# Score constants computed in the keys stage, and keys carried in rounds of three, three and two pieces

## The chip, the cores and the metric

One core of a Trainium2 chip runs the kernel. The metric is the device time of one execution in microseconds, as the median of three runs. The engines are TensorE (PE in the rows, PEld for its weight loads), VectorE (DVE), ScalarE (ACT), GpSimd (POOL) and SyncE (SP), which here issues nearly all DMAs.

## What is computed

A graph attention layer over 128 graphs with 128 nodes and 512 features, of which the first 20 nodes are the keys, with 16 heads of 32 features, in two directions:

```python
vcq = concatenate([v, q_exp], axis=-1)      # q_exp: the graph's condition, zero where a node's row sums to zero
self_feat = vcq @ W_self.T + b_self
for d in range(2):
    A = adj_f if d == 0 else swapaxes(adj_f, 1, 2)
    A = A[:, :, :20, :]
    cond, vb = A.sum(-1), A @ w_bias + b_bias
    kv = self_feat[:, :20]
    qh = (self_feat @ Wq[d].T + bq[d]).reshape(B, N, H, 32)
    kh = (kv @ Wk[d].T + bk[d]).reshape(B, 20, H, 32)
    aff = einsum('bnhd,bmhd->bnhm', qh, kh) / sqrt(32)
    aff = where(cond[:, :, None, :] > 0, aff, NEG) + vb[:, :, None, :]
    w = softmax(aff, axis=-1)
    out_t = einsum('bnhm,bmf->bnhf', w, kv)
    output += einsum('bnhf,hgf->bnhg', out_t, Wout[d]) + bout[d]
return v + relu(output)
```

## The kernel before

Three stages follow each other.

**prepare_weights** (to about 80 us) loads and turns the weights. It folds the query projection into the key side: a_rows holds, for each of 8 units (direction d, group of four heads), the product of Wself and Wq, and cq and bq_all hold what the graph's condition and the bias add to the query of each feature.

**keys_and_values** (about 80 to 372 us) makes the keys and values of all graphs in 8 halves of 16 graphs (320 columns: 16 graphs x 20 keys). Halves 2 to 5 run in a hardware loop (blocks), the others are written out. Per half PE makes 16 projections of 12 matmuls (8 key pieces, 8 value pieces), and between them the sums (8 matmuls) and the four features (48) of the next half. Results go to six PSUM banks in turn: a bank is free when its reader is through (free). ACT empties a key piece into kst, which has two buffers (key_out, L768), and SP stores it to k_dram (L634); ACT empties a value piece into vst (L778, L781), DVE turns it (L703) and SP stores it in four DMAs to v_dram (L640). DVE makes the next half's features (features_out, L669), ACT their high parts (feature_high, L755), POOL their low parts (features_low, L729); DVE turns the nodes of the half after next (turn_x, L75). SP's order in a half is: 8 loads of rows for the half after next (L70), 8 stores of keys, 32 stores of values. In the last half but one, the loads of rows give way to the first loads of the next stage (early_loads).

**window_loop** works off 64 pairs of graphs in slots of some 23 us. A window spans four pairs (8 graphs, 160 columns of keys for a group of heads). In each slot PE generates the mixed keys of two groups of heads for the next window, and computes the scores of four pairs of different age against the present one. generate(t, step) has five steps of 8 matmuls with 32 rows of weights; step 0 (L1540) makes the constants of the scores, from zl, which holds cq and bq_all by columns, and steps 1 to 4 (L1542) the four pieces of the mixed keys. Each step fills the same columns of the four low banks, so these must be emptied before the next: constants_high (ACT, L1432) and constants_low (DVE, L1267) into zc, keys_out (ACT, L1437) into kx. scores(t, a) multiplies the turned nodes xt by kx (L1562) and flags by zc (L1563). Then follow masks on DVE (L1280), maxima, POOL's shift, exponentials on ACT, sums (L1297), normalising, the turn of the weights on PE (turn_weights, L1588; read out by weights_out, L1450), values (L1596) and self_features (L1575). Pair t - 3 is called soft, pair t - 4 late, pair t + 1 nxt. The order of work in a slot is written out by hand for each engine. On PE it is: scores(3), generate 0, scores(2), generate 1, values, scores(1), turn_mask, generate 2, self_features, generate 3, flags, values, scores(0), generate 4, self_features. A matmul in float32 stands in the trace as two records, one in float32r as one.

## Time and profile before

| | us |
|---|---|
| median of three runs | 1914.61 |
| lowest, highest | 1913.51, 1915.31 |
| profiled execution | 1915.0 |
| its span, first to last instruction | 1913.2 |

PE is busy for 1864.9 us of the span, DVE for 1103.0, ACT for 1005.8 and POOL for 725.4. The ends of matmuls are modelled, so the distance from one start to the next tells what a matmul costs, not its length in the row. Idle time of an engine counts only where another waits for it. The mean granted clock of PE is 0.986 of 2.4 GHz.

### The profile page before, as it was taken

How to read it: one execution, taken by the hardware profiler on the slowest of the kernel's cores; microseconds unless marked ns; L12 is line 12 of the kernel's file. 1: busy time of each engine (PE TensorE's matmuls, PEld its weight loads, DVE VectorE, ACT ScalarE, POOL GpSimd, SP SyncE). 2: the span in 40 equal slices, each digit the busy share in tenths (PEclk: the TensorE clock that was granted, in tenths of full speed). 3: DMA queues.
4: the chain of work that ended last, by engine and by line, in shares of the span. 5: the costliest groups of instructions: out<-in, count | busy, mean ns of one | idle time of the engine just before them, and what ended most of it. 6: DMA issues, size and time to landing. Idle time of an engine off the chain costs nothing.

```text
span 1913.2 us, 46955 instructions
## 1 busy us (share of the span) xinstructions
PE 1864.9 (97%) x15864; PEld 1668.7 (87%) x15864; DVE 1103.0 (58%) x1937; ACT 1005.8 (53%) x1717; POOL 725.4 (38%) x617
## 2 busy tenths in 40 slices
PE   8999998879999999999999999999999999999997
PEld 5899998868888888888888888888888888888886
DVE  2433232456666666666666666666666666666632
ACT  2333232235556666666565566555666666656543
POOL 0322222004444444444444444444444444444444
PEclk9999999979999999999999999999999999999999
DMA  6123334444546565555555555565565555555431
GB/s 198 46 83 89 91 96 104 110 115 141 155 137 159 144 156 144 149 144 144 144 144 145 144 157 151 152 154 147 143 159 146 152 142 147 144 145 145 120 93 63
DMA packets 263747, 255.59 MB, mean 134 GB/s; under 512 B 78192, under 2 KB 194160, under 8 KB 263536
## 3 DMA queue, kind: packets, MB, share of 16 engines
q1 hardware_dynamic: 259360, 252.84, 49.4%
q8 instruction: 123, 2.02, 0.4%
q14 instruction: 88, 0.72, 0.1%
q10 hardware_dynamic: 4176, 0.02, 0.1%
HBM read 197.94 MB, written 54.79 MB: 132 GB/s over the span
## 4 chain that ended last, share of the span: by engine, by line
PE 92%; SPq 1%; DVE 1%; issue 1%; ACT 1%; DMA 0%; POOL 0%; POOLq 0%; DVEq 0%; ACTq 0%
PE bank L1562 30%; PE bank L1575 20%; PE low_banks L1542 10%; PE low_banks L828 9%; PE bank L1596 8%; PE bank L828 4%; PE bank L1588 4%; PE low_banks L1540 3%; PE bank L1563 2%; PE bank L1604 1%; SPq L640 1%; ACT kx L1437 0%; DVE zc L1267 0%; DMA k_dram<-kv_kst 0%; SPq L1078 0%
## 5 line engine op out<-in xcount | busy, mean ns | idle before, releaser
L1562 PE MATMUL bank<-kx,xt_main 128*128 128x160 f32 x4096 | 635.9, 304 | 0.3 <-ACT kx L1437 0.3
L1562 PEld LDWEIGHTS bank<-kx,xt_main 128*128 128x128 f32 x4096 | 583.8, 192 | 7.4 <-issue 0.9
L1437 ACT ACTIVATE kx<-low_banks 128x1280 f32<-128x1280 f32 (+3 forms) x268 | 318.2, 1187 | 259.1 <-PE low_banks L1542 259.1
L1388 POOL TENSOR_TENSOR res<-res,xk 128x512 f32<-128x512 f32 x128 | 163.9, 1280 | 669.6 <-ACT res L1427 669.6
L1280 DVE TENSOR_TENSOR sc<-bank,masks 128x320 f32<-128x320 f32 x256 | 125.8, 491 | 398.8 <-PE bank L1563 396.9
L1542 PE MATMUL low_banks<-key_tile,a_rows 32*128 32x160 f32 (+3 forms) x4288 | 220.7, 320 | 14.6 <-ACT kx L1437 8.9
L1575 PE MATMUL bank<-ws_h,xh_main 128*128 128x512 f32 x512 | 222.2, 434 | 2.5 <-DVE res L1306 2.5
L1370 POOL TENSOR_TENSOR sc<-sc,mx 128x640 f32<-128x640 f32 x128 | 160.2, 1272 | 152.1 <-DVE mx L1292 152.1
L1432 ACT ACTIVATE zc<-low_banks 128x1280 fp32r<-128x1280 f32 (+2 forms) x67 | 79.7, 1190 | 244.3 <-PE low_banks L1540 244.3
L1575 PE MATMUL bank<-ws_l,xh_main 128*128 128x512 f32 x512 | 203.1, 397 | 0.0
L1575 PE MATMUL bank<-ws_h,xl_main 128*128 128x512 f32 x512 | 203.0, 397 | 0.0
L1542 PEld LDWEIGHTS low_banks<-key_tile,a_rows 32*128 32x128 f32 x4288 | 157.9, 187 | 51.6 <-DVE zc L1267 16.4
L1364 POOL TENSOR_TENSOR xl_main<-xt_main,xh_main 128x512 fp32r<-128x512 f32 x128 | 162.7, 1271 | 55.1 <-ACT xh_main L1416 55.1
L1563 PE MATMUL bank<-zc,flags 128*128 128x160 f32 x512 | 177.9, 348 | 0.0
L1596 PE MATMUL bank<-vbd,wtt 128*128 128x128 f32 x1280 | 173.9, 283 | 3.8 <-ACT wtt L1450 3.7
L1379 POOL TENSOR_TENSOR wt<-sc,rs 128x640 f32<-128x640 f32 x128 | 163.0, 1273 | 14.1 <-DVE rs L1299 13.6
L1450 ACT ACTIVATE wtt<-bank 128x384 f32<-128x384 f32 (+1 forms) x256 | 111.5, 435 | 108.0 <-PE bank L1588 105.2
L1596 PEld LDWEIGHTS bank<-vbd,wtt 128*128 128x128 f32 x1280 | 152.9, 192 | 15.2 <-issue 14.5
L1306 DVE TENSOR_TENSOR res<-bank,res 128x512 f32<-128x512 f32 x128 | 88.5, 691 | 133.8 <-PE bank L1596 133.8
L75 DVE STREAM_TRANSPOSE xt_main<-rows_main 128x256 f32<-128x256 f32 x256 | 142.8, 619 | 0.0
L1575 PEld LDWEIGHTS bank<-ws_h,xh_main 128*128 128x128 f32 x512 | 96.6, 189 | 38.5 <-issue 20.6
L828 PE MATMUL low_banks<-kv_fh,wkv_h 128*128 128x320 f32 x352 | 110.3, 313 | 7.6 <-ACT kv_kst L768 4.9
(144 smaller groups left out, 3085.4 us busy)
## 6 DMA issues: line engine op xcount, KB each, us to landing
rows_main<-in_x SPq DMA_DIRECT2D x256, 128.0 KB, 6.3
xs<-in_x SPq DMA_DIRECT2D x64, 512.0 KB, 4.8
xk<-in_x SPq DMA_DIRECT2D x64, 512.0 KB, 3.7
res<-c_dram SPq DMA_DIRECT2D x64, 512.0 KB, 7.2
out<-res SPq DMA_DIRECT2D x128, 256.0 KB, 3.1
adj<-in_mask_BxSxSx_ik SPq DMA_DIRECT2D x32, 440.0 KB, 8.2
adj<-in_mask_BxSxSx_ik SPq DMA_DIRECT2D x128, 110.0 KB
vbd<-v_dram SPq DMA_DIRECT2D x768, 10.0 KB
```

The source lines that it names most:

```text
L75: return eng.transpose(dst, src.rearrange("p t (r j) -> p t r j", j=NQ)[:, :, :, j])
L828: mm = nc.tensor.matmul(dst, a(j), b(j), start=(j == 0 and k == 0), stop=(j == C - 1 and k == 2))
L1364: pool.tensor_tensor(xl[:, :, b, :], xt[:, :, p.ring + b, :], xh[:, :, b, :].bitcast(F32), ALU.subtract).then_inc(x_low, 1)
L1370: pool.tensor_tensor(s, s, mx[:, b, :].unsqueeze(2).to_broadcast([P, DIRS * H, NG]), ALU.subtract).then_inc(s_shifted, 1)
L1379: pool.tensor_tensor(wt[:, b, :].rearrange("p (h m) -> p h m", m=NG), sc[:, p.ring + b, :].rearrange("p (h m) -> p h m", m=NG), rs[:, b, : ...
L1388: pool.tensor_tensor(res[:, p.par, b, :], res[:, p.par, b, :], xk[:, p.par, b, :], ALU.add).then_inc(res_ready, 1)
L1437: nc.scalar.activation(taken(kx[:, t.par, j], lo, hi), generated(0, P, lo, hi), ACT.Copy).then_inc(gen_taken, 1)
L1542: mm = nc.tensor.matmul(low_banks[:, r, dst], a_rows[s, o, step - 1, :], rhs, start=True, stop=True)
L1562: mm = nc.tensor.matmul(dst, xt[:, j, p.ring + b, :], kx[:, t.par, j, :, :, w, :].rearrange("p r c m -> p c r m"), start=(j == 0), stop=False)
L1563: mm = nc.tensor.matmul(dst, flags[:, p.ring + b, :], zc[:, t.par, :, :, w, :].rearrange("p r c m -> p c r m"), start=False, stop=True)
L1575: mm = nc.tensor.matmul(OUT[:], a, m[:, j, :], start=(j == 0 and k == 0), stop=False)
L1596: mm = nc.tensor.matmul(OUT[:, 3 * c * DH:(3 * c + SLOTS) * DH], wtt[:, b, c, :], vbd[:, p.par, c, :, b * DH:b * DH + DH], start=False, st ...
```

## The change

The constants of the scores are linear in the keys: per head, the key times the query's bias, and the key times the condition's part of the query, summed over the head's 32 features. The changed kernel computes them in keys_and_values from kst: ACT multiplies a key piece by bq_all (by_biases), POOL by cq (by_conditions), DVE turns both products in blocks of 32 and sums over the 32 features (constant_sums), ACT and POOL split the sums of a half into high and low parts (constants_high, constants_low), DVE turns them (turn_constants), and SP stores them in 8 DMAs per half to z_dram. In the window loop SP loads two small pieces of z_dram per pair into zc (load_constants); flags and nzm follow zc's new layout.

generate has three rounds instead of five steps: pieces 0 to 2, 3 to 5 (12 matmuls each) and 6 and 7 (8 matmuls), where a piece is one of the eight of two groups of heads. The turn of the masks moves ahead of the round of two, place_masks behind weights_out. scores waits for all three rounds at its opening. Of the early loads, those of the edges, of the two edge constants and of xs (load_sum_rows) move to the last half, ahead of its third key store (late_loads), and DVE treats direction 1 of the first edges in the window loop.

```diff
             for p in range(NK):
+                if last and p == 2:
+                    sp.wait_ge(pe_feat, C * HALVES)
+                    sp.wait_ge(f_low, C * HALVES)
+                    v["late_loads"](sp)
...
+            sp.wait_ge(z_turned, n + 1)
+            for r in range(NQ):
+                for e in range(2):
+                    o = Q * r + ZQ * e
+                    sp.dma_start(v["z_dram"][r, e::2, bass.ds(n * HALF, HALF)].rearrange("c (q i) -> q c i", i=Q),
+                                 zt[o:o + MQ]).then_inc(z_stored, 16)
...
+        def constant_sums(n, p):
+            dve.wait_ge(by_bias, NK * n + p + 1)
+            dve.wait_ge(by_condition, NK * n + p + 1)
+            if due(NK * n + p):
+                dve.wait_ge(z_summed, NK * n + p)
+            nc.vector.transpose(pt[:], prod[:, p % 2].rearrange("p k (q i) -> p (k q) i", i=Q)).then_inc(p_turned, 1)
+            dve.wait_ge(p_turned, NK * n + p + 1)
+            if p == 0 and due(n):
+                dve.wait_ge(z_high, n)
+                dve.wait_ge(z_low, n)
+            nc.vector.tensor_reduce(zs[:, p].rearrange("p k q -> p (k q)"), pt[:], AX.X, ALU.add).then_inc(z_summed, 1)
...
                 pick_condition(n + 1)
-            if not last:
                 nonzero(n + 1, 1 - par)
-                for j in range(C):
+            constant_sums(n, 0)
+            for j in range(C):
+                constant_sums(n, 1 + j)
+                if not last:
                     features_out(n + 1, 1 - par, j)
+            constant_sums(n, 5)
             if not tail:
                 turn_x(blk + 1, n + 2, par)
...
                 nc.vector.transpose(vt[:, m % 4], vst[:, m % 2]).then_inc(v_turned, 1)
+                if m < 2:
+                    constant_sums(n, 6 + m)
+            turn_constants(n)
...
+        def by_conditions(n, p):
+            pool.wait_ge(kv_out, 2 * NK * n + p + 1)
+            if due(NK * n + p - 1):
+                pool.wait_ge(p_turned, NK * n + p - 1)
+            pool.tensor_tensor(prod[:, p % 2, 1, :].rearrange("p (b m) -> p b m", m=NG),
+                               kst[:, p % 2, :].rearrange("p (b m) -> p b m", m=NG),
+                               cq[:, p, bass.ds(n * HB, HB)].unsqueeze(2).to_broadcast([P, HB, NG]),
+                               ALU.mult).then_inc(by_condition, 1)
...
         def one_half(blk, n, par, first, last, tail):
+            by_conditions(n, 0)
+            by_conditions(n, 1)
             if not last:
                 conditions(n + 1)
-                features_low(n + 1, 1 - par)
+            for j in range(C):
+                by_conditions(n, 2 + j)
+                if not last:
+                    feature_low(n + 1, 1 - par, j)
+            by_conditions(n, 6)
+            by_conditions(n, 7)
             if not tail:
                 x_lows(n + 2, par)
+            constants_low(n)
...
+            if due(NK * n + p - 1):
+                act.wait_ge(by_condition, NK * n + p - 1)
+                act.wait_ge(by_bias, NK * n + p - 1)
             nc.scalar.activation(kst[:, p % 2, :], slot_bank(par, PROJ_SLOT[p]), ACT.Identity, scale=SCALE,
                                  bias=bk_s[:, p:p + 1]).then_inc(kv_out, 1)
+        def by_biases(n, p):
+            act.wait_ge(kv_out, 2 * NK * n + p + 1)
+            if due(NK * n + p - 1):
+                act.wait_ge(p_turned, NK * n + p - 1)
+            nc.scalar.activation(prod[:, p % 2, 0, :], kst[:, p % 2, :], ACT.Copy,
+                                 scale=bq_all[:, p:p + 1]).then_inc(by_bias, 1)
...
             for j in range(C):
                 key_out(n, par, j)
+                by_biases(n, j)
             for j in range(C):
                 key_out(n, par, C + j)
+                by_biases(n, C + j)
                 if not last:
                     feature_high(n + 1, 1 - par, j)
...
+    ROUNDS = ((0, 1, 2), (3, 4, 5), (6, 7))
...
+    def late_loads(sp):
+        sp.dma_start(wb[:], v["w_bias"].partition_broadcast(P)).then_inc(edge_consts, 16)
+        sp.dma_start(bb[:], v["b_bias"].partition_broadcast(P)).then_inc(edge_consts, 16)
+        load_edges(sp, 0, 0)
+        load_sum_rows(sp, Pair(0, 0))
+        load_edges(sp, 0, 1)
...
+    def load_constants(sp, p):
+        for b in range(2):
+            o = (2 * p.n + b) * NG
+            sp.dma_start(zc[ZK * b:ZK * b + ZK, p.c % AGES, :].bitcast(F32).rearrange("k (h m) -> k h m", m=NG),
+                         v["z_dram"][:, :, bass.ds(o, NG)].rearrange("r (p k) m -> k (r p) m", k=ZK)
+                         ).then_inc(zc_loaded[p.par], 16)
...
-        def generate(t, step):
+        def generate(t, g):
             d, hh = unit(t)
             lo, hi = window(t)
-            if step == 0:
+            if g == 0:
                 pe.wait_ge(key_loaded[t.par], 16 * (t.half + 1))
-                pe.wait_ge(zl_ready, 2 * (t.n + 1) if t.real() else 2 * PAIRS)
-                if due(t.n):
-                    pe.wait_ge(gen_taken, C * t.n)
-            elif step == 1:
-                pe.wait_ge(z_low, t.n + 1)
-            else:
-                pe.wait_ge(gen_taken, C * t.n + step - 1)
-            for c in range(2):
-                o = C * d + 2 * hh + c
+            if due(NR * t.n + g):
+                pe.wait_ge(gen_taken, NR * t.n + g)
+            for i, u in enumerate(ROUNDS[g]):
+                j, c = u // 2, u % 2
                 for r in range(NQ):
                     s = slice(Q * r, Q * r + Q)
-                    rhs = key_tile[s, t.par, c, lo * NG:hi * NG]
-                    dst = slice(c * UN + lo * NG, c * UN + hi * NG)
-                    if step == 0:
-                        mm = nc.tensor.matmul(low_banks[:, r, dst], zl[s, o, :], rhs, start=True, stop=True)
-                    else:
-                        mm = nc.tensor.matmul(low_banks[:, r, dst], a_rows[s, o, step - 1, :], rhs, start=True, stop=True)
+                    mm = nc.tensor.matmul(low_banks[:, r, i * UN + lo * NG:i * UN + hi * NG],
+                                          a_rows[s, C * d + 2 * hh + c, j, :],
+                                          key_tile[s, t.par, c, lo * NG:hi * NG], start=True, stop=True)
             mm.then_inc(pe_gen, 1)
         def scores(t, a):
             p = t.back(a)
             n = scored(t, a)
+            d, hh = unit(t)
+            o = C * d + 2 * hh
+            zu = zc[:, p.c % AGES, :].rearrange("k (r p m) -> k p r m", r=NQ, m=NG)[:, o:o + 2]
             opening = a == ages(t)[0]
             if opening:
-                pe.wait_ge(gen_taken, C * t.n + C - 1)
+                pe.wait_ge(gen_taken, NR * t.n + NR)
             if a == 0:
                 pe.wait_ge(x_turned, C * (p.n + 1))
                 pe.wait_ge(e_out, p.n + 1)
+                pe.wait_ge(zc_loaded[p.par], 32 * (p.half + 1))
             if due(n - 2):
...
-            if has_window(nxt):
-                generate(nxt, 0)
...
             if has_window(nxt):
-                generate(nxt, 1)
+                if t.c % 2 == 1 and t.back(1).real():
+                    pe.wait_ge(mask_set, 2 * (t.back(1).half + 1))
+                generate(nxt, 0)
             if late.real():
                 values(late, 1)
             if t.back(1).real():
                 scores(t, 1)
-            if t.c % 2 == 0 and t.real():
-                turn_mask(t)
             if has_window(nxt):
-                generate(nxt, 2)
+                generate(nxt, 1)
             if soft.real():
                 self_features(soft, 0, range(0, 2))
                 turn_weights(soft, 0, 0)
                 self_features(soft, 0, range(2, C))
                 turn_weights(soft, 0, 1)
+            if t.c % 2 == 0 and t.real():
+                turn_mask(t)
             if has_window(nxt):
-                if t.c % 2 == 0 and t.real():
-                    pe.wait_ge(mask_set, 2 * (t.half + 1))
-                generate(nxt, 3)
+                generate(nxt, 2)
...
-            if has_window(nxt):
-                generate(nxt, 4)
```

Where the instructions stand, engine by engine.

PE in the window loop, from the scores of the opening age to the third set of mixed keys, in one steady slot. Before (key_tile is the keys of the window, zl and a_rows the weights of constants and mixed keys, wt the softmax weights that are turned, vbd the values):

```order
L1540 MATMUL low_banks<-key_tile,zl 128x160 x8
L1588 MATMUL bank<-identity,wt 128x128 x3
L1562 MATMUL bank<-kx,xt_main 128x160 x4
L1563 MATMUL bank<-zc,flags 128x160
L1562 MATMUL bank<-kx,xt_main 128x160 x4
L1563 MATMUL bank<-zc,flags 128x160
L1588 MATMUL bank<-identity,wt 128x128 x2
L1542 MATMUL low_banks<-key_tile,a_rows 128x160 x8
L1596 MATMUL bank<-vbd,wtt 128x128 x5
```

The same place in the changed kernel (its L1647 and L1650 are the scores, L1675 the turn of the weights, L1683 the values, L1623 the rounds of generate):

```order
L1675 MATMUL bank<-identity,wt 128x128 x3
L1647 MATMUL bank<-kx,xt_main 128x160 x4
L1650 MATMUL bank<-zc,flags 128x160
L1647 MATMUL bank<-kx,xt_main 128x160 x4
L1650 MATMUL bank<-zc,flags 128x160
L1675 MATMUL bank<-identity,wt 128x128 x2
L1623 MATMUL low_banks<-key_tile,a_rows 128x160 x12
L1683 MATMUL bank<-vbd,wtt 128x128 x5
```

The eight matmuls of the constants ahead of the weights' turn are gone, and twelve of mixed keys stand where eight stood.

ACT in the keys stage, from the fourth key piece of a half to its first value piece, in the last block written out; kv_kst is a key piece, kv_fh the high part of the next half's features. Before:

```order
L768 ACTIVATE kv_kst<-bank,bk_s 128x320
L755 ACTIVATE kv_fh<-kv_fs 128x320
L768 ACTIVATE kv_kst<-low_banks,bk_s 128x320
L755 ACTIVATE kv_fh<-kv_fs 128x320
L768 ACTIVATE kv_kst<-low_banks,bk_s 128x320
```

The changed kernel (L853 the key pieces, L861 the new product with the bias, L837 the high parts):

```order
L853 ACTIVATE kv_kst<-bank,bk_s 128x320
L861 ACTIVATE kv_prod<-kv_kst,bq_all 128x320
L837 ACTIVATE kv_fh<-kv_fs 128x320
L853 ACTIVATE kv_kst<-low_banks,bk_s 128x320
L861 ACTIVATE kv_prod<-kv_kst,bq_all 128x320
L837 ACTIVATE kv_fh<-kv_fs 128x320
L853 ACTIVATE kv_kst<-low_banks,bk_s 128x320
```

Each key piece is followed by its product, ahead of the high parts.

DVE in the keys stage, from the next half's last features to the end of the half, changed kernel (L698 the features, L717 and L722 constant_sums, L75 turn_x, L756 the values' turn, L729 turn_constants); before, the same row held the features, the four L75 and then the eight turns of values (L703) and nothing else:

```order
L698 SCALAR_TENSOR_TENSOR kv_fs<-low_banks,cb,kv_rc 128x10x32
L717 STREAM_TRANSPOSE kv_pt<-kv_prod 128x640
L722 TENSOR_REDUCE kv_zs<-kv_pt 128x20
L75 STREAM_TRANSPOSE nodes_t<-rows 128x320 x4
L756 STREAM_TRANSPOSE kv_vt<-kv_vst 128x512
L717 STREAM_TRANSPOSE kv_pt<-kv_prod 128x640
L722 TENSOR_REDUCE kv_zs<-kv_pt 128x20
L756 STREAM_TRANSPOSE kv_vt<-kv_vst 128x512
```

A pair of the new instructions now stands ahead of turn_x and one between the first two turns of values.

## Rows read from the trace of the kernel before

**Rows 1.** Busy time and share by engine, and the chain that ended last.

```profile
PE 1864.9 (97%) x15864; PEld 1668.7 (87%) x15864; DVE 1103.0 (58%) x1937; ACT 1005.8 (53%) x1717; POOL 725.4 (38%) x617
...
PE 92%; SPq 1%; DVE 1%; issue 1%; ACT 1%; DMA 0%; POOL 0%; POOLq 0%; DVEq 0%; ACTq 0%
```

**Rows 2.** Busy by stretch: PE, PEld, DVE, ACT, POOL, clock, DMA share, GB/s.

```profile
320.00:325.00 5.00, 5.00 (x23) 5.00 (x22) 0.07 (x1) 1.67 (x4) 1.08 (x2) 0.57 0.23 80
...
600.00:1200.00 600.00, 600.00 (x5396) 530.35 (x5389) 395.30 (x700) 360.65 (x594) 257.76 (x206) 1.00 0.57 148
```

**Rows 3.** Timeline of PE, keys stage: start, length, instruction, idle before.

```profile
318.90 0.64 PE L828 MATMUL low_banks<-kv_fh,wkv_h 128*128 128x320 f32 x1 [4.86 <-ACT kv_kst L768]
```

**Rows 4.** Timeline of ACT, keys stage.

```profile
229.63 0.53 ACT L768 ACTIVATE kv_kst<-low_banks,bk_s 128x320 f32<-128x320 f32 x1 [1.15 <-PE low_banks L828]
240.29 0.53 ACT L768 ACTIVATE kv_kst<-low_banks,bk_s 128x320 f32<-128x320 f32 x1 [10.13 <-DMA k_dram<-kv_kst]
...
243.25 0.46 ACT L755 ACTIVATE kv_fh<-kv_fs 128x320 fp32r<-128x320 f32 x1
...
318.32 0.53 ACT L768 ACTIVATE kv_kst<-low_banks,bk_s 128x320 f32<-128x320 f32 x1 [15.44 <-DMA k_dram<-kv_kst]
```

**Rows 5.** Timeline of SP's queue, keys stage.

```profile
106.01 13.98 SPq L640 DMA_DIRECT2D v_dram<-kv_vt  x32
...
215.41 15.88 SPq L640 DMA_DIRECT2D v_dram<-kv_vt  x32
232.02 6.00 SPq L70 DMA_DIRECT2D rows<-in_x  x8
238.29 11.13 SPq L634 DMA_DIRECT2D k_dram<-kv_kst  x8
251.77 15.48 SPq L640 DMA_DIRECT2D v_dram<-kv_vt  x32
```

**Rows 6.** Timeline of PE in a steady slot of the window loop.

```profile
1013.01 0.82 PE L1540 MATMUL low_banks<-key_tile,zl 32*128 32x160 f32 x16
1013.77 0.55 PE L1588 MATMUL bank<-identity,wt 128*128 128x128 f32 x3
1014.15 1.25 PE L1562 MATMUL bank<-kx,xt_main 128*128 128x160 f32 x8
...
1015.32 1.28 PE L1562 MATMUL bank<-kx,xt_main 128*128 128x160 f32 x8
...
1022.09 0.50 PE L1575 MATMUL bank<-ws_h,xh_main 128*128 128x512 f32 x1
1022.42 0.40 PE L1575 MATMUL bank<-ws_l,xh_main 128*128 128x512 f32 x1
1022.65 0.40 PE L1575 MATMUL bank<-ws_h,xl_main 128*128 128x512 f32 x1
```

**Rows 7.** Timeline of PE in the tail, a step of 40 columns.

```profile
1867.75 0.65 PE L1540 MATMUL low_banks<-key_tile,zl 32*128 32x40 f32 x16
1868.33 0.55 PE L1588 MATMUL bank<-identity,wt 128*128 128x128 f32 x3
```

**Rows 8.** Line L1540 from 600 to 1800 us: ns min/median/max, first and last start.

```profile
L1540 PE MATMUL low_banks<-key_tile,zl x816: 294/294/398, 618.8 to 1778.9; 32*128 32x160 f32 x164
```

**Rows 9.** Timeline of SP's queue: the key loads that open two slots following each other.

```profile
1013.97 0.37 SPq L1088 DMA_DIRECT2D key_tile<-k_dram  x1
...
1032.45 0.37 SPq L1088 DMA_DIRECT2D key_tile<-k_dram  x1
```

**Rows 10.** Timelines of DVE and POOL: keys stage, first masks, and a reduction.

```profile
250.89 0.71 DVE L703 STREAM_TRANSPOSE kv_vt<-kv_vst 128x512 f32<-128x512 f32 x1 [1.94 <-ACT kv_vst L778]
...
396.22 0.49 DVE L1280 TENSOR_TENSOR sc<-bank,masks 128x320 f32<-128x320 f32 x1 [5.21 <-PE bank L1563]
...
1017.15 0.81 DVE L1297 TENSOR_REDUCE sm<-sc 128x32 f32<-128x640 f32 x1
...
247.68 0.89 POOL L729 TENSOR_TENSOR kv_fl<-kv_fs,kv_fh 128x320 fp32r<-128x320 f32 x1 [2.18 <-ACT kv_fh L755]
```

More of the change, by code:

```diff
@@ L141, in build @@
         kv_out = sem("kv_out")
+        z_stored = sem("z_stored")
         with ExitStack() as third:
-            windowed, early_loads, early_turn = window_loop(nc, scope(third)[0], sem, bank, low_banks, locals())
+            windowed, early_loads, late_loads, early_turn = window_loop(nc, scope(third)[0], sem, bank, low_banks, locals())
         with ExitStack() as keyed:
@@ L1260, in vector_program @@
     def vector_program(dve):
-        def constants_low(t):
-            dve.wait_ge(z_high, t.n + 1)
-            lo, hi = window(t)
-            o = taken(zc[Q:ZR, t.par], lo, hi)
-            nc.vector.tensor_tensor(o, generated(Q, ZR, lo, hi), o.bitcast(F32), ALU.subtract).then_inc(z_low, 1)
+        nc.vector.memset(zc[:].bitcast(F32), 0.0).then_inc(set_once, 1)
+        nc.vector.memset(nzm[:], 0.0).then_inc(set_once, 1)
+        dve.wait_ge(set_once, 2)
+        for b in range(2):
+            for o in (0, 2):
+                nc.vector.memset(nzm[:, b::2, ZK * b + o:ZK * b + o + 1], 1.0).then_inc(set_once, 1)
         def add_masks(t, a):
@@ L1309, in slot @@
             soft, late = t.back(3), t.back(4)
-            nxt, after = t.back(-1), t.back(-2)
+            nxt = t.back(-1)
             if soft.real():
@@ L1333, in slot @@
                 nonzero_rows(dve, nxt)
-            if after.real():
-                condition_columns(dve, after)
             g = edge_group(t if t.c % 2 == 0 else t.back(1))
-            if due(g) and has_edges(g):
+            if has_edges(g) and (due(g) or t.c % 2):
                 count_and_weigh(dve, g, t.c % 2)
```

174 lines of the change are left out of this document (93 added, 81 removed).

## Prediction

> **What bounds the kernel now.** I read the page's engine shares and its chain first: TensorE (PE) is busy for 97% of the span and the chain that ended last runs 92% on it [rows 1]. The table by stretch then says where: from 600 to 1200 us PE is busy for every microsecond at full clock, ScalarE (ACT) for 361 and VectorE (DVE) for 395 of 600 [rows 2]. So in the window loop a matmul that goes is time that goes, and work of the other engines is free until one of them becomes late. The keys stage (some 80 to 372 us) is PE's too, except for one hole: PE stands 4.86 us at 318.9 for a bank that ACT had not emptied [rows 3], and the 5 us behind it show a granted clock of 0.57, so near the lower of its two levels, 1.2 GHz [rows 2]. That hole has to be read with the rows of SyncE (SP) and ACT, because the change puts its new work exactly there.
>
> How near the keys stage is to such a hole everywhere: ACT's key_out(2) of a half starts at 240.29, 10.66 us after key_out(1) at 229.63 [rows 4]. It waited for k_dram's store of piece 0, which SP could issue only at 238.29, behind 32 stores to v_dram (15.88 us) and 8 loads of rows (6.00 us) [rows 5]. At the hole the same pair was 15.97 us apart (318.32, less 15.44 of idle and 0.53 of work: 302.35 [rows 4]) and PE ran dry at 318.90 - 4.86 = 314.0, which is 11.7 us after key_out(1). So PE can bear 11.7 us; it gets 10.66 plus 0.53 for key_out(2) itself. The slack is about half a microsecond per half.
>
> **The window loop: what goes.** Step 0 of generate (the constants' 8 matmuls, 16 records on PE) is gone in each of 67 windows, and four steps of 16 records become rounds of 24, 24 and 16. One step costs 0.76 us from its first start to the next instruction's [rows 6], and the next wide matmul is served 0.33 us before its follower where 0.23 is usual [rows 6], so about 0.84 in all. What part of that belongs to the step and what to its matmuls? Nine score records of the same 160 columns, with all 128 rows, take 1.17 us, 0.13 each [rows 6]; four row groups of 32 run side by side, so 16 records stream for 4 x 0.13 = 0.52, and 0.32 is fixed. The tail has steps with a quarter of the columns, and they still take 0.58 [rows 7]: so a step is far from free of a fixed part. Before: 5 x 0.84 = 4.2 us per window. After: 64 records = 2.08, and three fixed parts = 0.96, so 3.04. **Saving 1.16 us** of a slot of (1778.9 - 618.8) / 50 = 23.2 us [rows 8], for the 63 windows behind the ramp: **-73 us**. If the fixed part really goes with each record (as the short step would also allow), only a fifth of 4.2 goes: 0.84, -53 us. If the weight of a switch is larger than I read, at most 1.3, -82 us. I take 1.16, since the full-width rows are the ones that the change alters.
>
> The Trainium skill bears on this choice ("TensorEngine Tiling (Array Packing)", Key Properties): a change of tiling mode drains TensorE. By that rule the fixed part is a property of each entry into the 32-row mode and there are two entries fewer, the -73; without it the sum would be made with -53. The 0.33 behind a round beside the usual 0.23 agrees with it.
>
> Does something take PE's place in the loop? ACT empties the banks in three pieces instead of five, with a fifth fewer elements, DVE loses constants_low (1.48 us) and the column copies. SP gets two loads of zc per slot, at some 0.4 to 0.5 us each by the issue time of its other loads. It now has 18.5 us of work per slot (1013.97 to 1032.45, where the next slot's keys are issued) [rows 9], so 19.5 in a slot of 22.1: it keeps up. The loads go out at the start of SP's slot and are wanted by scores(t, 0) some 20 us later. scores(t, 3) now waits for all three evictions, but between round 2 and it lie values, scores(t, 0) and 12 self_features, 7 us. Round 1 follows round 0 after 3.6 us of other matmuls, ACT's eviction of 1920 elements needs about 1.7 plus 0.3. The tightest is turn_weights(soft, 0, 1): it wants weights_out, now behind the longer keys_out(1); by adding up ACT's slot it is 0.2 us early. Cost zero; if it is late, some tenths per slot, up to +15 us in all.
>
> **The keys stage: what comes.** Per half (8 key pieces) ACT gets 8 by_biases of 128x320 (0.46, as the feature_high of the same shape [rows 4]), GpSimd (POOL) 8 by_conditions (0.87 to 0.89, as feature_low [rows 10]), DVE 8 transposes of 128x640 (0.71 for 512 columns [rows 10], so 0.85) and 8 reductions (0.81 [rows 10]), and SP 8 stores to z_dram. In sum ACT +4 us, POOL +7, DVE +13, SP +3.6 in a half of 36.4 us: every engine would have room. But they stand in the queues between things that wait for each other, and that is what I price.
>
> Take T, the start of key_out(2). Now: feature_high(0) at T+2.96, right behind key_out(4) [rows 4], the first transpose of values (vt) at 250.89 = T+10.6 [rows 10]. Changed: by_conditions(3+j) on POOL stands behind feature_low(j), which waits for ACT's feature_high(j), which stands behind key_out(4+j) and by_biases(4+j); and key_out(5+j) waits for by_conditions(3+j), since kst has two buffers. That is a ring: 0.53 + 0.46 + 0.46 + 0.87 + 0.87 and five hand-overs of 0.1 = 3.7 us per turn, where PE delivers a piece every 1.76 or 3.5. Three turns: key_out(7) at T+2.6+11 = T+13.7, DVE's last constant_sums of the row ends at T+15.3, four turn_x (2.7), and vt starts at about **T+18.3, 7.7 us later** than now. From vt on SP's row is fixed: 0.88 to its first v_dram store (250.89 to 251.77), 22.88 from there to the first k_dram store (215.41 to 238.29 [rows 5]), 2.0 until that has landed and key_out(2) starts (240.29): 25.8. With today's 10.6 that is 36.4, just PE's own half (248 matmuls, the two v_dram starts 36.36 apart). The eight z_dram stores stand in that row too, at 0.45 each (v_dram's: 15.88 / 32 = 0.50 in the loop, 13.98 / 32 = 0.44 outside [rows 5]): +3.6. So the half becomes 18.3 + 25.8 + 3.6 = **47.7 us against PE's 36.4**: PE waits some 11 in each of the halves of the hardware loop. Without the ring, with the z stores alone, 10.6 + 25.8 + 3.6 = 40.0, less the half microsecond of slack: +3 per half.
>
> Summed over the halves: half 0 hands over without a stall before it, so half 1 pays about 4; halves 2 to 5 pay 11 each, 44; half 6, behind one loop half, 10; half 7, whose row on SP has the cheap stores and no loads of rows, about 6. Together 64. Off it goes what vanishes: the old hole, 4.9, and its slow clock, 2.4 less the same behind the last hole: -5. The loads of edges (880 KB) leave the place where they held up the k_dram store, but come back in the last half before its third store; that holds ACT by some 3 us there, behind PE's last hole. **+59 us.** Bounds: +15 if the ring doesn't bind (3 x 6, less 5, and 2 for the loads), +80 if hand-overs cost 0.2 each and z stores 0.6. The clock loss behind the other holes costs nothing: the ring and SP set the half, PE only fills it.
>
> **Between the stages.** Now PE's last projection ends at 371.5 and the first masks are added at 396.22 [rows 10], behind the load of xs of pair 0. Changed: xs of pair 0 comes early, but SP ends its z stores some 18 us behind PE (early_turn stands before the last vt on DVE), then issues xs of pair 1, whose row_sums stand ahead of ACT's keys_out(1) of slot 0, and of flag_rows: first scores some 8 us later. The four short windows lose two trips PE-ACT-PE each, about 2 us apiece: -8. **Sum 0**, between -8 and +8.
>
> **Sum.** Span 1913.2, its execution 1915.0, the median of the three runs 1914.6. 1915.0 - 73 + 59 + 0 = **1901 us**.
>
> **Rivals.** (a) The rounds save only by record, not by step: -53. With the rest as above 1915 - 53 + 59 = 1921, **slower** by 0.3%. It decides where a window saves less than 0.94 us (59 / 63): below that the keys stage costs more than the loop gives back. For it: the short step's 0.58 of 0.76; against: the late start behind each round. With it goes the case that ring or SP cost more than 59 (hand-overs of 0.2, 72 us): 1915 - 73 + 72 = 1914, and both together 1934. (b) The ring doesn't bind, because PE's own rate lets ACT and POOL run ahead: then only SP's 3.6 is over the slack, +15, and the time is 1915 - 73 + 15 = 1857. For it: each engine's share is low; against: kst has two buffers, so ACT cannot run ahead of POOL by more than a piece. (c) The constants don't leave the path but come back as a wait for zc_loaded in scores(t, 0): with 20 us between issue and use I see no way for it, except in slot 0. (d) ACT is late for turn_weights by 0.2 us per slot: 1901 + 13 = 1914, no change.
>
> **How the numbers follow.** The forecast (1888 to 1916) gets 0.55; (a) with its companion 0.22; (b) and what lies between it and the forecast 0.13; (d) 0.10. A measurement of this kernel tells 0.2%, 3.8 us, from no change. Faster by more than that, below 1911: four fifths of the forecast, all of (b), a bit of (d), 0.61. Within: 0.16. Slower, above 1918: most of (a), 0.23. The range from 1880 to 1928 leaves out the far end of (b) and of (a), some 2 in 10.
>
> **What would show it.** In the changed trace: a round of 24 records takes 1.0 to 1.05 us to the next start and the slot 22.1; if 1.14 (1.5 x 0.76), (a). In the keys stage PE waits of about 8 to 11 us for kst's key_out, one per half from the third on, ACT's wait before key_out(2) some 18 us long for k_dram, and halves 47 to 48 us apart; if PE shows no waits there, (b). PE's last projection near 430 instead of 371. It is wrong if the sequence of DVE's constant_sums lets vt start near T+11, if z stores take far from 0.45, or if the loop shows waits of PE for wtt or zc.

## The result and the profile after

| | before | changed |
|---|---|---|
| median of the runs, us | 1914.06 (1911.7 to 1915.31, 4 runs) | 1887.61 (1882.65 to 1889.68, 4 runs) |
| span of the profiled execution, us | 1913.2 | 1887.9 |

Changed over before: 0.9859, with a 95% interval of 0.9838 to 0.9881. The change makes the kernel 1.4% faster; the forecast was 1901 us, 0.7%. Both opposite effects that the forecast named are there, and the time lies 13 us under the forecast.

The page of the changed kernel, busy time and shares of the chain (before: [rows 1]):

```profile
PE 1790.1 (95%) x14792; PEld 1629.0 (86%) x14792; DVE 1117.5 (59%) x1879; ACT 953.2 (50%) x1655; POOL 773.0 (41%) x689
...
PE 77%; issue 7%; SPq 7%; DVE 3%; POOL 3%; DMA 2%; ACT 1%; POOLq 0%; DVEq 0%; ACTq 0%
```

TensorE (PE) has 75 us less work, but its share of the chain falls from 92% to 77%: SyncE's queue (SPq), DVE and POOL have come onto the path, and "issue", time in which an engine waited for nothing that the profile shows. The table by stretch says where (columns as in [rows 2]):

```profile
320.00:325.00 5.00, 1.69 (x6) 1.69 (x7) 0.66 (x1) 2.07 (x4) 0.73 (x1) 0.50 0.40 131
600.00:1200.00 600.00, 600.00 (x5276) 541.03 (x5275) 382.90 (x661) 346.81 (x581) 273.73 (x219) 1.00 0.59 157
```

In the window loop PE is still busy for all of 600 us; in the keys stage it stands. PE's waits for a key piece from 75 to 420 us (total, times, longest), where before had one of 4.86 us [rows 3]:

```profile
PE low_banks L933 <- ACT kv_kst L853: 52.1, 7, 12.7
```

**The same half of the keys stage as in [rows 4, 5], changed.** SP's queue, then ACT, then DVE:

```profile
244.69 16.20 SPq L663 DMA_DIRECT2D v_dram<-kv_vt  x32
261.07 3.60 SPq L669 DMA_DIRECT2D z_dram<-kv_zt  x8
267.59 6.05 SPq L70 DMA_DIRECT2D rows<-in_x  x8
273.92 16.12 SPq L657 DMA_DIRECT2D k_dram<-kv_kst  x8
294.47 5.72 SPq L663 DMA_DIRECT2D v_dram<-kv_vt  x12
```

```profile
276.03 0.53 ACT L853 ACTIVATE kv_kst<-low_banks,bk_s 128x320 f32<-128x320 f32 x1 [22.23 <-DMA k_dram<-kv_kst]
...
281.81 0.53 ACT L853 ACTIVATE kv_kst<-low_banks,bk_s 128x320 f32<-128x320 f32 x1 [1.67 <-POOL kv_prod L799]
...
285.41 0.53 ACT L853 ACTIVATE kv_kst<-bank,bk_s 128x320 f32<-128x320 f32 x1 [1.67 <-POOL kv_prod L799]
...
289.00 0.53 ACT L853 ACTIVATE kv_kst<-low_banks,bk_s 128x320 f32<-128x320 f32 x1 [1.67 <-POOL kv_prod L799]
```

```profile
293.28 0.67 DVE L756 STREAM_TRANSPOSE kv_vt<-kv_vst 128x512 f32<-128x512 f32 x1
```

The prediction's row can be read off. key_out(2) starts at T = 276.03 after 22.23 us of idle time (forecast some 18); key_out(5), (6) and (7) follow 3.6 us apart (forecast 3.7), each behind POOL's product; vt comes at T+17.3 (forecast T+18.3) and the next v_dram stores at T+18.4 (forecast T+19.2). The eight z_dram stores take 3.60. The v_dram starts lie 49.8 us apart here (244.69 to 294.47), where SP's hardware loop turns back (last section), and 47.4 on the mean of the five intervals from the second to the seventh half; forecast 47.7.

**The window loop.** PE in a steady slot (before: [rows 6]): two rounds of 24 records with what follows, and the round of 16.

```profile
1001.59 0.82 PE L1623 MATMUL low_banks<-key_tile,a_rows 32*128 32x160 f32 x16
1002.35 0.29 PE L1691 MATMUL bank<-identity_b,nzm 128*128 128x128 bf16 x2
...
1014.21 1.10 PE L1623 MATMUL low_banks<-key_tile,a_rows 32*128 32x160 f32 x24
1015.29 1.35 PE L1683 MATMUL bank<-vbd,wtt 128*128 128x128 f32 x10
...
1018.66 0.34 PE L1650 MATMUL bank<-zc,flags 128*128 128x160 f32 x1
1018.93 1.10 PE L1623 MATMUL low_banks<-key_tile,a_rows 32*128 32x160 f32 x24
1019.96 0.51 PE L1662 MATMUL bank<-ws_h,xh_main 128*128 128x512 f32 x1
1020.30 0.40 PE L1662 MATMUL bank<-ws_l,xh_main 128*128 128x512 f32 x1
```

From first start to the follower's start 0.76, 1.08 and 1.03 us (forecast for 24 records 1.00 to 1.05).

**The bill.** ACT's flags_out runs once in every slot, 64 times, and cuts the loop. Its last 58 starts, before and changed (first and last start behind the colon):

```profile
L1462 ACT ACTIVATE flags<-bank x58: 377/377/378, 494.2 to 1816.1; 128x256 fp32r<-128x256 f32 x58
```

```profile
L1557 ACT ACTIVATE flags<-bank x58: 378/382/386, 543.0 to 1793.6; 128x256 fp32r<-128x256 f32 x58
```

(1816.1 - 494.2) / 57 = 23.19 us a slot before, (1793.6 - 543.0) / 57 = 21.94 changed. PE's projections into low_banks, first and last start, before and changed:

```profile
L828 PE MATMUL low_banks<-kv_fh,wkv_h x352: 307/308/636, 79.1 to 366.8; 128*128 128x320 f32 x176
```

```profile
L933 PE MATMUL low_banks<-kv_fh,wkv_h x352: 307/308/635, 76.6 to 425.6; 128*128 128x320 f32 x176
```

| stretch, us | before | changed | difference | forecast |
|---|---|---|---|---|
| start to first projection | 79.1 | 76.6 | -2.5 | 0 |
| first to last projection | 287.7 | 349.0 | +61.3 | +59 |
| to the first flags_out (380.6; 440.6) | 13.8 | 15.0 | +1.2 | } -3.5 |
| first to seventh flags_out (ramp) | 113.6 | 102.4 | -11.2 | } |
| 57 steady slots | 1321.9 | 1250.6 | -71.3 | } -69.6 |
| last flags_out to end | 97.1 | 94.3 | -2.8 | } |
| sum | 1913.2 | 1887.9 | -25.3 | -14 |

The forecast's -73 stands for 63 windows of 1.16 us. One of the 67 windows has its step 0 ahead of the first flags_out, six have it in the ramp's row, 57 in the steady slots and three behind them. So three of the 63 (3.5 us) belong to the ramp, beside the forecast's 0 between the stages, and 60 (69.6 us) to the last two rows.

### The profile page after: what moved, and what is told of

It reads as the page before. It is cut to its first block, busy times and chain, and to the rows that moved or that the text cites. A ratio compares the mean times of both kernels' runs of the same rounds, so it can differ in the third digit from the quotient of the medians.

```text
span 1887.9 us, 45438 instructions
## 1 busy us (share of the span) xinstructions
PE 1790.1 (95%) x14792; PEld 1629.0 (86%) x14792; DVE 1117.5 (59%) x1879; ACT 953.2 (50%) x1655; POOL 773.0 (41%) x689
## 4 chain that ended last, share of the span: by engine, by line
PE 77%; issue 7%; SPq 7%; DVE 3%; POOL 3%; DMA 2%; ACT 1%; POOLq 0%; DVEq 0%; ACTq 0%
PE bank L1647 30%; PE bank L1662 20%; PE low_banks L1623 9%; PE bank L1683 9%; PE bank L1675 4%; SPq L663 4%; PE bank L1650 2%; PE bank L486 1%; POOL kv_prod L799 1%; SPq L70 1%; SPq L669 1%; DMA k_dram<-kv_kst 1%; PE bank L1691 1%; DVE kv_pt L717 1%; DVE kv_vt L756 1%
## 5 line engine op out<-in xcount | busy, mean ns | idle before, releaser
L1647 PE MATMUL bank<-kx,xt_main 128*128 128x160 f32 x4096 | 632.7, 303 | 0.0
L1647 PEld LDWEIGHTS bank<-kx,xt_main 128*128 128x128 f32 x4096 | 581.5, 192 | 6.0 <-issue 0.3
L1532 ACT ACTIVATE kx<-low_banks 128x1920 f32<-128x1920 f32 (+5 forms) x201 | 306.2, 1524 | 43.1 <-PE low_banks L1623 43.0
L1662 PE MATMUL bank<-ws_h,xh_main 128*128 128x512 f32 x512 | 217.7, 425 | 3.5 <-DVE res L1410 3.4
L1623 PE MATMUL low_banks<-key_tile,a_rows 32*128 32x160 f32 (+3 forms) x4288 | 202.5, 315 | 7.6 <-ACT kx L1532 4.0
L1623 PEld LDWEIGHTS low_banks<-key_tile,a_rows 32*128 32x128 f32 x4288 | 155.2, 188 | 36.2 <-issue 20.2
L1650 PE MATMUL bank<-zc,flags 128*128 128x160 f32 x512 | 177.4, 346 | 0.0
L1683 PE MATMUL bank<-vbd,wtt 128*128 128x128 f32 x1280 | 172.9, 282 | 4.3 <-ACT wtt L1545 4.1
L1683 PEld LDWEIGHTS bank<-vbd,wtt 128*128 128x128 f32 x1280 | 153.6, 192 | 17.0 <-issue 16.6
L933 PE MATMUL low_banks<-kv_fh,wkv_h 128*128 128x320 f32 x352 | 114.7, 326 | 54.4 <-ACT kv_kst L853 52.1
L75 DVE STREAM_TRANSPOSE xt_main<-rows_main 128x256 f32<-128x256 f32 x256 | 142.6, 620 | 0.0
L1537 ACT ACTIVATE sc<-sc 128x640 f32<-128x640 f32 x128 | 93.8, 733 | 91.2 <-POOL sc L1470 91.2
L717 DVE STREAM_TRANSPOSE kv_pt<-kv_prod 128x640 f32<-128x640 f32 x64 | 53.4, 834 | 134.4 <-POOL kv_prod L799 133.1
```

The source lines that it names most:

```text
L75: return eng.transpose(dst, src.rearrange("p t (r j) -> p t r j", j=NQ)[:, :, :, j])
L1532: nc.scalar.activation(taken(t, j, lo, hi), generated(j, lo, hi), ACT.Copy).then_inc(gen_taken, 1)
L1623: mm = nc.tensor.matmul(low_banks[:, r, i * UN + lo * NG:i * UN + hi * NG], a_rows[s, C * d + 2 * hh + c, j, :], key_tile[s, t.par, c, lo ...
L1647: mm = nc.tensor.matmul(dst, xt[:, j, p.ring + b, :], kx[:, t.par, :, 2 * j:2 * j + 2, w * NG:w * NG + NG] .rearrange("p r c m -> p c r m" ...
L1650: mm = nc.tensor.matmul(dst, flags[:, p.ring + b, :], zu, start=False, stop=True)
L1662: mm = nc.tensor.matmul(OUT[:], a, m[:, j, :], start=(j == 0 and k == 0), stop=False)
```

## The experiments

All were timed against the kernel before, which stood at 1911.5 to 1913.5 us in them. A difference of two experiments is taken from their medians; each is known to about 3 us.

**1. Are the two halves of the change separate?** The keys stage without the new work:

```diff
                 key_out(n, par, j)
-                by_biases(n, j)
...
-            constant_sums(n, 0)
...
-            by_conditions(n, 0)
...
-            turn_constants(n)
...
-                    sp.dma_start(v["z_dram"][r, e::2, ...], zt[o:o + MQ]).then_inc(z_stored, 16)
```

> The changed kernel without the products, their sums, turns and stores in the keys stage; the window loop loads its constants from other values of the same shape (that part of the result is left out). Theory: the two halves of the change add up. The keys stage goes back to the 36.4 us a half of before, the window loop keeps its 21.93 us a slot: 1887.6 - 60.9 (keys stage) - 0 to 4 (the stretch behind it) = 1823 to 1827 us, 4.7% under the kernel before. Rival: part of the window loop's gain (the 12.6 us between first masks and slot 4) came only because its loads had more time behind a longer keys stage: then those 12.6 us come back and the time is about 1838 us.

The diff leaves out the lines that follow from these. Measured: 1811.8 us, ratio 0.9478 (0.9462 to 0.9494), 75.8 less than the changed kernel. The slot is 21.94 as in the changed kernel, so the loop's gain does not depend on what stands ahead of it. The work costs more than the 61 us of the bill, since the change also takes something out of the keys stage:

```profile
L906 PE MATMUL low_banks<-kv_fh,wkv_h x352: 307/308/468, 75.7 to 357.3; 128*128 128x320 f32 x176
```

281.6 us from first to last projection, 6.1 less than before: the loads of edges no longer stand ahead of the k_dram stores, and the hole of [rows 3] is gone. So the new work costs 349.0 - 281.6 = 67.4 there; 4.1 more go up to the first flags_out (10.9 to 15.0) and 6.3 in the ramp (96.1 to 102.4).

**2. SP's stores alone.** As 1, with the eight z_dram stores a half left in, from a tile that DVE turns once a half.

> The changed kernel without the products, their sums and what ACT and POOL did for them, but with the eight z_dram stores a half (of a tile of zeros, turned once a half by DVE): the constants are zeros, that part of the result is left out. It prices SP's stores alone, over the kernel without products (1811.8 us). By the prediction's bound (3.6 us a half over a slack of half a microsecond, in six halves, that is 3 a half): 18 us, 1830 us. Theory now, from the changed kernel against the one without z stores: a store costs the same with and without the ring, 26 to 31 us, 1838 to 1843 us. Rival, without products SP's queue still has its slack and the stores cost nothing: 1812 us.

Measured: 1839.8 us, 28.0 over the kernel of 1; 24.4 of it in the keys stage:

```profile
L914 PE MATMUL low_banks<-kv_fh,wkv_h x352: 304/308/636, 75.6 to 381.6; 128*128 128x320 f32 x176
```

That is 3.5 us for each of the seven halves that have another behind them, but it is not spread evenly. From one half's first v_dram store to the next, the seven intervals are 0.0, 0.4, 4.6, 8.5, 4.4, 3.9 and 2.6 us longer than in the kernel of 1. In the first two the slack still hides the stores. From then on PE stands for key_out (17.8 us in five waits), and behind such a wait it works at a lower granted clock for some us. 48 records of PE on the chain, at full clock and behind the wait before 204.92, and the row by stretch there (clock 0.81):

```profile
97.89 7.04 PE low_banks L914 x48
204.92 8.84 PE low_banks L914 x48
```

```profile
204.90:213.70 8.80, 8.78 (x49) 8.78 (x50) 3.28 (x5) 3.07 (x7) 2.33 (x3) 0.81 0.23 78
```

So, by estimate from these rows, a half pays the stores less the slack, and 1.8 us of clock on top; the 8.5 is the half in which SP's loop turns back (last section). The prediction's lower bound, 3 in six halves, was too low by these two things, neither of which was tried by itself.

**3. The products alone.** The changed kernel without the z_dram stores, all else as it is.

> The changed kernel with the products, sums and turns but without the 64 z_dram stores of SP (eight a half, 3.4 us a half); the constants are loaded from other values, so that part of the result is left out. Theory (ring of two key buffers, and SP's queue, one behind the other in one loop): about 24 us come back, 3.6 a half over the halves that wait, half 43.8 us, time about 1864 us. Rival one, stores alone are the cause: the halves go back to 36.4 us and the time to about 1827 us. Rival two, the ring alone is the cause and the stores lie beside it: the half stays at 47 us and the time at 1888 us.

Measured: 1856.0 us, 31.6 under the changed kernel and 44.2 over the kernel of 1.

```profile
L925 PE MATMUL low_banks<-kv_fh,wkv_h x352: 304/308/636, 75.7 to 394.2; 128*128 128x320 f32 x176
```

In the keys stage the products cost 318.5 - 281.6 = 36.9, the stores 24.4, both together 67.4. The two add up to 61.3 of the 67.4: one row of queues, each pushing the next. Both single-cause rivals fall.

**4. Four key buffers.**

```diff
-    kst = sb("kv_kst", [P, 2, HALF], F32)
+    kst = sb("kv_kst", [P, 4, HALF], F32)
...
-            if due(NK * n + p - 1):
-                act.wait_ge(by_condition, NK * n + p - 1)
+            if due(NK * n + p - 3):
+                act.wait_ge(by_condition, NK * n + p - 3)
```

> The changed kernel with four key buffers in place of two (key_out waits for the product, and for the store, of four keys ago). Theory (ring): key_out no longer waits for the product of two keys ago, the turn of 3.6 us falls back, about 3 us a half come back: half 44.8 us, time 1864 us (-23). Rival, SP alone: its queue of row loads, stores of keys, values and constants is the whole of the lengthening; half 47 us, 1888 us.

Measured: 1863.7 us, -23.9. The size is as expected, but the reason is another. ACT in a half of this kernel:

```profile
266.96 0.53 ACT L853 ACTIVATE kv_kst<-low_banks,bk_s 128x320 f32<-128x320 f32 x1 [16.99 <-DMA k_dram<-kv_kst]
267.60 0.56 ACT L861 ACTIVATE kv_prod<-kv_kst,bq_all 128x320 f32<-128x320 f32 x1
...
271.12 0.56 ACT L861 ACTIVATE kv_prod<-kv_kst,bq_all 128x320 f32<-128x320 f32 x1 [2.19 <-DVE kv_pt L717]
```

by_biases still come 3.52 us apart: the turn has not fallen back, it is held by the two product buffers instead. What four buffers give is that key_out(2) and (3) no longer wait for a store; only key_out(4) does (the row at 266.96), and fewer turns are left behind it.

**5. Where SP's stores stand.** z_dram stores of a half behind the key stores of the next; key stores 0 to 3 ahead of the eight row loads; both; both with four buffers.

```diff
+            for p in range(first_keys):
+                key_store(n, p)
...
             sp.wait_ge(x_turned, C * (n + 1))
             load_half_rows(sp, v, n + 2, par, loaded[par])
-            for p in range(NK):
+            for p in range(first_keys, NK):
                 key_store(n, p)
+            sp.wait_ge(z_turned, n)
+            z_stores(n - 1)
...
-            sp.wait_ge(z_turned, n + 1)
-            z_stores(n)
```

> The changed kernel with the z_dram stores of each half issued behind the eight key stores of the next half (and those of the last half at the end), all else as it was. Theory: the stores cost because they stand between the last value store of a half and the row loads and first key store of the next, which ACT's key_out waits for; behind the key stores SP has time, and nearly all that came back without the stores comes back: 1856 to 1862 us. Rival, SP has no time left anywhere in a half and every store costs its issue: 1888 us.

> The changed kernel with key stores 0 to 3 of a half issued ahead of the eight row loads of SP (6.0 us), z_dram stores as in the changed kernel, two key buffers. Theory: the wait of ACT's key_out(2) for the store of piece 0 ends 6 us earlier; a half 44 us, 26 to 30 us less than the changed kernel: 1858 to 1862 us; with z_late's 25 together about the 53 that both gave, so the row loads and the z stores stand in one line and add up. Rival: the row loads, now later, make turn_x and x_cast of the half after next late, and half of the gain is lost: 1873 us.

> The changed kernel with the z_dram stores late as in z_late, and with key stores 0 to 3 of a half issued before the eight row loads of SP instead of behind them. Theory (the first key stores, on which both key buffers hang, wait behind row loads and z stores): both go, half 36 to 38 us, 52 us less than the changed kernel: 1836 us. Rival, the ring of two key buffers (3.6 us a key) stays the limit: the gain is that of z_late alone, 1856 to 1862 us.

> The changed kernel with z stores late, key stores 0 to 3 ahead of the row loads, and four key buffers. Theory: nothing of ring and queue is left, the half is PE's 36.4 us as in the kernel before, what is left over the kernel without products is its last half: 1815 to 1822 us, 5% under the kernel before. Rival, what ACT, DVE and POOL do for the products (1.1 + 1.9 + 0.9 us a key and more) delays the features of the next half whatever the buffers: half 40 us, 1840 us.

| kernel | us | against before | against changed | first to last projection, us |
|---|---|---|---|---|
| z stores late | 1862.6 | 0.9743 (0.9727 to 0.9760) | -25.0 | 325.2 |
| first four key stores early | 1859.2 | 0.9721 (0.9702 to 0.9739) | -28.4 | 321.5 |
| both | 1834.8 | 0.9598 (0.9582 to 0.9614) | -52.8 | 298.4 |
| both and four key buffers | 1821.4 | 0.9529 (0.9513 to 0.9545) | -66.2 | 280.8 |

Not one instruction was taken away for these times, and 25.0 + 28.4 = 53.4 is, within the error, what both give together (52.8). So row loads and z stores cost because they stand in one line ahead of the store that key_out(2) waits for. In the last kernel the line is gone:

```profile
252.87 15.76 SPq L679 DMA_DIRECT2D v_dram<-kv_vt  x32
268.90 2.55 SPq L640 DMA_DIRECT2D k_dram<-kv_kst  x4
271.72 6.00 SPq L70 DMA_DIRECT2D rows<-in_x  x8
277.97 4.54 SPq L640 DMA_DIRECT2D k_dram<-kv_kst  x4
282.69 3.63 SPq L647 DMA_DIRECT2D z_dram<-kv_zt  x8
288.31 1.71 SPq L679 DMA_DIRECT2D v_dram<-kv_vt  x4
```

```profile
238.06 0.56 ACT L874 ACTIVATE kv_prod<-kv_kst,bq_all 128x320 f32<-128x320 f32 x1
...
241.59 0.57 ACT L874 ACTIVATE kv_prod<-kv_kst,bq_all 128x320 f32<-128x320 f32 x1 [1.21 <-DVE kv_pt L730]
...
245.15 0.56 ACT L874 ACTIVATE kv_prod<-kv_kst,bq_all 128x320 f32<-128x320 f32 x1 [1.25 <-DVE kv_pt L730]
```

The v_dram starts lie 35.4 us apart there (252.87 to 288.31; 36.9 on the mean of the first six intervals), and the keys stage is as short as without any product (280.8 against 281.6), though the products still turn at 3.5 us. That is PE's own pace where a projection and a features product alternate. So a turn of 3.5 us costs nothing by itself; it costs when it starts late, because then PE's pieces that have piled up can't be taken faster than one in 3.5 us. With the same order and only two key buffers (the kernel "both") this holds for halves 0 to 5, in which PE waits 1.8 us in all for key pieces; in the last two, where loads for the next stage still stand ahead of key stores, it waits 11.5.

**6. Rounds of two pieces.** The changed kernel's loop with one round more:

```diff
-    ROUNDS = ((0, 1, 2), (3, 4, 5), (6, 7))
+    ROUNDS = ((0, 1), (2, 3), (4, 5), (6, 7))
...
                 scores(t, 0)
+            if has_window(nxt):
+                generate(nxt, 3)
```

> The changed kernel with the keys carried in four rounds of two pieces (8 matmuls) in place of 3, 3 and 2; the fourth stands behind the scores of age 0, as in the kernel before. Theory, a step costs by its entry and exit: four rounds of 0.76 us = 3.04 against 1.08 + 1.03 + 0.76 = 2.87, and one more entry of 0.08 and exit of 0.10 us: 0.35 us a window, 67 windows, +23 us: 1911 us. Rival, a step costs by its matmuls alone, 32 in both: 1888 us, within 3 us.

Measured: 1930.0 us, ratio 1.0090 (1.0072 to 1.0109): +42.3 on the changed kernel where 23 were expected, and slower than before. The slot and one place in it:

```profile
L1557 ACT ACTIVATE flags<-bank x58: 377/381/386, 544.2 to 1831.9; 128x256 fp32r<-128x256 f32 x58
```

```profile
1007.36 0.83 PE L1625 MATMUL low_banks<-key_tile,a_rows 32*128 32x160 f32 x16
1008.44 1.35 PE L1687 MATMUL bank<-vbd,wtt 128*128 128x128 f32 x10 [0.26 <-ACT wtt L1545]
```

```profile
1007.29 0.74 ACT L1537 ACTIVATE sc<-sc 128x640 f32<-128x640 f32 x1 [1.33 <-POOL sc L1470]
1007.93 0.37 ACT L1545 ACTIVATE wtt<-bank 128x256 f32<-128x256 f32 x1
```

(1831.9 - 544.2) / 57 = 22.59, 0.65 more a slot. 0.26 of it is a wait that the changed kernel doesn't have: values(late, 1) stands for the turned weights, which ACT copies behind its exponentials, which wait for POOL. With three pieces the round is 0.3 us longer and covers it. The other 0.39 is one more entry: 4 x 0.76 = 3.04 against 2.87, and the late start ahead of and behind it. The division is known to about 0.06: by starts alone values(late, 1) comes 1.08 us behind the round's start instead of 0.76, so the wait moves it by 0.32, and 0.33 is left for the entry.

**7. Step 0 alone.** The kernel before without step 0 of generate and what served it:

```diff
                 if due(t.n):
                     pe.wait_ge(gen_taken, C * t.n)
+                return
...
-                constants_high(nxt)
...
-                constants_low(nxt)
...
-                condition_columns(dve, after)
```

> The kernel before with step 0 of generate taken out of the window loop, its eight matmuls a window and what made and took its data (condition_columns and constants_low on DVE, constants_high on ACT); the constants are zeros, so that part of the result is left out. Keys stage unchanged, steps 1 to 4 as they were. Theory (from the run with rounds of two): the step's 0.76 us go and 0.14 us at its neighbours, but values(late,1) then comes 0.32 us too early for ACT's copy of the turned weights and PE waits there: 0.58 us a window, 67 windows, 39 us: 1873 us, with about 0.3 us of PE's waits a slot at values. Rival, nothing waits and the step is worth its whole 0.90 us: 60 us, 1852 us. Rival, the saving is by matmuls (a quarter of a step of 32 matmuls of 3.0 us): 50 us, 1862 us, and no waits.

Measured: 1860.4 us, ratio 0.9736 (0.9716 to 0.9756): -52.3, where the theory said -39. The wait is there as it said, over 1100 us of the loop:

```profile
PE bank L1587 <- ACT wtt L1446: 12.6, 49, 0.3
```

```profile
L1458 ACT ACTIVATE flags<-bank x58: 377/378/378, 476.2 to 1763.2; 128x256 fp32r<-128x256 f32 x58
```

(1763.2 - 476.2) / 57 = 22.58 a slot: 0.61 saved (expected 0.58), and the same slot as in 6, which was reached from the other side. What the theory missed is the ramp: first to seventh flags_out takes 97.8 us instead of 113.6. The rows of this stretch, before and without step 0 (columns as in [rows 2]), and two of PE's waits in it that only the kernel before has:

```profile
380.60:494.20 113.60, 100.31 (x936) 89.08 (x937) 68.65 (x126) 58.64 (x99) 27.60 (x22) 0.87 0.46 128
378.40:476.20 97.80, 88.69 (x840) 79.12 (x841) 58.63 (x106) 52.16 (x94) 27.52 (x22) 0.94 0.55 149
```

```profile
PE low_banks L1542 <- DVE zc L1267: 4.6, 4, 2.3
PE low_banks L1540 <- ACT kx L1437: 2.7, 3, 1.2
```

Six steps 0 are gone from it (96 records). PE stands 9.1 us instead of 13.3, so 4.2 of the 15.8 are waits. The other 11.6 are busy time: six steps at 0.76 us are 4.6 of it, and the remaining 7 go with the granted clock, which is 0.94 here where it was 0.87. This last division is an estimate from these rows.

## Why the prediction was right, and where it was not

**The window loop, -73: right in kind, and 4.5 us too small.** Its share in the last two rows of the bill is -69.6, and they came out at -74.1. A steady slot saves 1.25 us, not 1.16; the last three windows gave 2.8, not 3.5. By 6 and 7 step 0 costs about 0.87 (0.61 and the wait of 0.26 that its absence opens when nothing else fills it) and an entry about 0.39, where the prediction had 0.84 and 0.32; with the wait taken as 0.32 they are 0.93 and 0.33, and the sum is the same. The fixed part goes with the entry and not with the record: rival (a), in which the kernel would have been slower, is refuted, since the kernel of 6 has the same records and one more round, and a slot of it is 0.65 us longer, of which the wait is at most 0.32. The Trainium skill ("TensorEngine Tiling (Array Packing)", Key Properties) says that a change of tiling mode drains TensorE; the price of each entry in 6 agrees with it, though no row shows the drain itself.

**"Cost zero" beside it: right by luck.** The prediction checked ACT against turn_weights(soft, 0, 1) and did not look at values(late, 1). There, without step 0, PE comes 0.26 us too early; the round of three pieces happens to fill just that. Rival (d) had the right kind of wait at the wrong place, with about the right size; in the changed kernel the steady slots show none.

**The keys stage, +59: right within 2.3 us,** with the row that it gave: turn 3.6, vt at T+17.3, stores 3.6, half 47.4. Its account of the parts was worse than its sum. The stores alone, put at 3 a half, cost 3.5 on the mean and between 0 and 8.5 (2); and "ring" is a name for a late start, not for a rate (4 and 5). That the lower clock behind the holes costs nothing holds in the changed kernel, where the longest pieces of the chain from 240 to 300 us are SP, POOL, DVE and ACT and none is PE's; with the stores alone it did cost (2). What left the stage gave 6 us, where the prediction had 5. Rival (b), in which the products lie beside PE's work, falls with PE's 52 us of waits; rival (c) too, since no wait for the loads of zc shows in the loop.

**Between the stages, 0: the step that failed.** With the ramp's three windows of the loop's term, -3.5 was forecast here, and it came out at -10.0 (+1.2 and -11.2). The +8 was right in kind, since with the products these stretches take 4.1 + 6.3 = 10.4 more than without. The wait can be seen at the loads of xs for pair 1, issued behind the z stores:

```profile
449.98 0.63 ACT L1553 ACTIVATE xs<-xs 128x512 f32<-128x512 f32 x1 [6.83 <-DMA xs<-in_x]
```

```profile
452.22 0.40 PE L1699 MATMUL low_banks<-identity,m1r 80*128 80x80 f32 x1 [7.43 <-ACT kx L1532]
```

The "-8, about 2 us apiece" for the four short windows was the mis-sized term: without the products these stretches change by -20.4 (-2.9 up to the first flags_out, -17.5 in the ramp), of which 3.5 was forecast in the loop's term, so it stands at -16.9. Step 0 alone is 15.8 of the 20.4 (7). The prediction counted two trips to another engine and back in each of four windows. The runs show a smaller part in waits (4.2 of the 15.8 in 7), and a larger one in PE's busy time, which the prediction left out: the steps' own matmuls, and the lower granted clock at which PE worked in the ramp. How the remaining 4.6 divide between fewer rounds and the other order of the loads was not tried.

**The first 80 us, -2.5:** the code there is that of before up to the end of the weights, and in experiment 7, where all of it is the kernel before, the first projection starts at 75.9; over all runs it lies between 75 and 79 us. This is scatter, and no part of the change.

Together -6.5 between the stages, -4.5 in the loop, -2.5 and +2.3 make the 11.3 us between -14 and -25.3, but for rounding.

## What to carry over

Price a step that leaves a pipeline twice: in the steady state, where it may hide a wait (0.61 us a slot here), and in the ramp, where its round trip through other engines lies open and the bound engine runs at a lower granted clock (15.8 us over six slots here). Ahead of adding stores to a queue, look for the one store in it that frees a buffer: here the order of issue alone was worth 53 us, and with two more buffers the change gave 4.7% instead of 1.4%. And a handover ring at the bound engine's own pace was harmless here as long as it started on time.

## What had not been expected of the hardware

SP's hardware loop over the keys halves turns back once. With no z_dram stores in its body the gap at this place was 0.74 us (231.22 + 16.24 = 247.46 to 248.20 in experiment 3), and with the eight more a half it was 2.9 us: 261.07 + 3.60 = 264.67 to 267.59 in the rows of the changed kernel above. The chain of the changed kernel has this gap as a piece in which SP waited for nothing that the profile shows:

```profile
264.84 2.46 issue
```

All kernels of this case agree: the four with 96 DMA issues in the body have a gap of 0.7 us, the eight with 112, wherever the z stores stand in it, of 2.9 to 3.2. So the longer body goes with a turn that is dearer by 2.2 us or more; why was not tried.

An entry of PE into the 32-row matmuls costs, by starts, 0.42 us where a 128x512 matmul follows, against the 0.33 to 0.39 that experiment 6 gives: 0.22 inside (16 records 0.76, 24 records 1.03, so 0.27 for eight), 0.09 ahead (the round starts 0.27 behind the last score record, other records 0.18), and 0.11 behind (0.34 to the second matmul instead of 0.23).
